# Attention and ternary FFN sandwich on one core: a second pair's bias written into PSUM by VectorE in place of ScalarE

## What is computed

```
x = x + layernorm(attention(layernorm(x)))
x = x + layernorm(ffn(layernorm(x)))

attention: qkv = x @ W_qkv + b_qkv; 16 heads of 8 dims
  scores = q k^T / sqrt(8) + rel_bias[clip(i - j + 128, 0, 256)]   (per head)
  out = softmax(scores) @ v, then @ W_out + b_out
ffn: h = silu(x w1^T s1) * (x w2^T s2); h = gelu(h h1^T s); h = gelu(h h2^T s); h w3^T s
```

## Time and profile before

| what | us |
|---|---|
| median of 3 executions | 339.37 |
| lowest and highest | 337.92, 339.51 |
| the profiled execution: its time | 338.78 |
| the profiled execution: its span in the trace | 337.0 |
| TensorE busy | 282.9 (84%) |
| ScalarE busy | 220.1 (65%) |
| VectorE busy | 210.0 (62%) |
| GpSimd busy | 49.8 (15%) |

### The profile page before, as it was taken

How to read it: one execution, slowest core, us unless ns; L and a number is a source line. 1 busy time by engine, 2 the same in 40 slices (tenths; PEclk the granted TensorE clock), 3 DMA queues, 4 the chain that set the end, 5 groups by cost and what they waited for, 6 DMA issues and landing times.

```text
span 337.0 us, 4914 instructions
## 1 busy us (share of the span) xinstructions
PE 282.9 (84%) x1778; PEld 181.2 (54%) x1778; DVE 210.0 (62%) x444; ACT 220.1 (65%) x315; POOL 49.8 (15%) x51
## 2 busy tenths in 40 slices
PE   0787979999999899999989967838788997999960
PEld 0454545455555465555555533425567876788840
DVE  4666644425967869686785945923857733655454
ACT  1297056447688795987879699615594867687640
POOL 6302300000100101000010137201403200401011
PEclk9999555559999999999999995585997999999995
DMA  6955891102222052341312000000000000010102
GB/s 163 372 179 139 241 330 19 58 15 80 66 65 93 21 177 63 102 153 42 90 32 66 3 1 2 0 5 0 1 0 2 0 0 0 2 31 1 33 1 62
DMA packets 22731, 22.85 MB, mean 68 GB/s; under 512 B 4017, under 2 KB 19505, under 8 KB 22449
## 3 DMA queue, kind: packets, MB, share of 16 engines
q1 hardware_dynamic: 19872, 19.16, 18.6%
q10 hardware_dynamic: 2832, 3.34, 3.1%
HBM read 15.93 MB, written 6.29 MB: 66 GB/s over the span
## 4 chain that ended last, share of the span: by engine, by line
PE 46%; DVE 24%; ACT 12%; issue 8%; SPq 6%; DMA 3%; POOL 1%; POOLq 0%; ACTq 0%; DVEq 0%
PE place L1066 8%; DVE mx L514 8%; PE place L1067 8%; PE place L918 6%; PE pv L966 6%; ACT ring L744 5%; PE place L910 3%; SPq L340 3%; DVE stats L461 3%; ACT place L751 3%; PE place L944 3%; DVE place L521 2%; PE pv L1067 2%; PE pv L1066 2%; DVE y_and_z L472 2%
## 5 line engine op out<-in xcount | busy, mean ns | idle before, releaser
L514 DVE TENSOR_REDUCE mx<-place 128x4 f32<-128x1024 f32 x64 | 78.2, 1223 | 43.3 <-PE place L918 43.3
L744 ACT ACTIVATE ring<-place 128x1024 f32<-128x1024 f32 x64 | 65.2, 1020 | 6.3 <-PE place L955 4.5
L751 ACT COPY place<-raw 128x1024 f32<-128x1024 f32 x48 | 48.8, 1016 | 18.1 <-DVE mx L514 18.1
L918 PE MATMUL place<-room,identr 128*128 128x512 f32 x128 | 54.0, 507 | 0.0
L406 POOL TENSOR_TENSOR rstd<-mv,mhalf 128x2 f32<-128x2 f32 (+1 forms) x24 | 20.4, 848 | 206.4 <-DVE mv L469 206.4
L944 PE MATMUL place<-room 33*128 33x256 f32 x256 | 36.3, 365 | 6.7 <-ACT place L751 4.3
L966 PE MATMUL pv<-ring,vx 128*9 128x256 f32 x512 | 38.7, 426 | 1.0 <-ACT ring L744 1.0
L1066 PE MATMUL place<-room,w_hi 128*128 128x512 f32 x96 | 38.6, 402 | 0.5 <-DVE room L623 0.5
L910 PE MATMUL place<-room 33*128 33x256 f32 x256 | 32.6, 335 | 7.6 <-ACT ring L744 5.2
L623 DVE TENSOR_TENSOR room<-ring,room 128x512 fp32r<-128x512 f32 x32 | 21.7, 691 | 26.2 <-ACT room L831 26.2
L1067 PE MATMUL place<-room,w_hi 128*128 128x512 f32 x96 | 37.7, 393 | 0.0
(11 more groups left out here) (97 smaller groups left out, 391.6 us busy)
## 6 DMA issues: line engine op xcount, KB each, us to landing
room<-q_parts SPq DMA_DIRECT2D x64, 64.0 KB
room<-k_parts SPq DMA_DIRECT2D x64, 64.0 KB
raw<-ext ACTq DMA_DIRECT2D x4, 768.0 KB, 8.0
w_lo<-h SPq DMA_DIRECT2D x2, 1024.0 KB, 5.1
k_parts<-z_parts SPq DMA_DIRECT2D x6, 256.0 KB, 3.1
k_parts<-w_hi SPq DMA_DIRECT2D x6, 256.0 KB, 3.9
xs<-x SPq DMA_DIRECT2D x4, 256.0 KB, 5.8
q_parts<-z_parts SPq DMA_DIRECT2D x4, 256.0 KB, 3.3
```

The costliest lines, as they stand in the source:

```text
L514: nc.vector.tensor_reduce(mx[:, s // RPAIRS, :, :, s % RPAIRS].rearrange("p i k -> p k i"), tile_of(b * PAIRS + s)[:, :, :].rearrange("p k ...
L744: nc.scalar.activation(probs[:, s % PRING, :, :, :].rearrange("p k j n -> p (k j n)"), tile_of(b * PAIRS + s)[:, :, :].rearrange("p k n -> ...
L751: nc.scalar.copy(tile_of(i)[:, :, :].rearrange("p k (j n) -> p k j n", j=2), pair_windows(raw[:, :, :], i % PAIRS)).then_inc(bias_set, 1)
L918: last = mm(tile_of(b * PAIRS + s)[:, half, :], identr[:, :], windows(table_hi[:, 2 * s + half, :], 0, P, 2, S), start=False, stop=True, s ...
```

## The change

Pair 2 of each batch joins pair 5: VectorE copies its bias, ScalarE does not. Everything else, TensorE's program, GpSimd's and the DMA queue's included, has the same instructions in the same order.

```
-BY_DVE = (5,)
+BY_DVE = (2, 5)
```

## The result

| | us |
|---|---|
| before, median of 6 executions | 339.53 (337.92 to 345.63) |
| changed, median of 6 executions | 331.53 (330.23 to 338.53) |
| ratio | 0.9756, 95% interval 0.9717 to 0.9795 |
| the changed kernel's profiled execution: time, span | 338.53, 336.7 |

The sign was right, the size was not: 8 us for the 2.5 forecast. One thing must be said to read any of these numbers: executions of either kernel fall into two groups some 6 us apart, and a median of six moves with the count in each.

A forecast was written before the change was run, and what follows sets the result against it. No engine is full; a loop of waits through ScalarE's copy of pair 2 sets the 20.19 us batch. Gains 1.4 + 0.2 + 0.95 = 2.5 us, from a mean of 338.9, give 336.4 us, range 334.6 to 338.9.

The forecast's parts named there:

- What VectorE has to bear: Slot 0 of a batch: the new 1.23 us copy fits VectorE's 1.40 us gap, 0.14 to spare, and costs nothing.
- What ScalarE wins: Batches 1 to 6: pair 1's exponential starts near 139.0, not 139.8; slot 2's maximum matmuls follow sooner, 0.27 us off TensorE's path.
- what is late next: Slot 4: maximum matmuls still wait for pair 3's exponential, so L540 waits for project; 0.23 us a batch remain, 1.4 for six.
- Batch 0: First batch, at half clock: the step from score to maximum matmuls shortens; gain taken as 0.2 us.
- Batch 7: Last batch, ScalarE full: the removed copy shortens the path by its full step, 0.95 us, bounds 0.33 and 1.0.
- only the ends gain: Rival, batches 1 to 6: another wait holds the period at 20.19; gain 0.95 + 0.2, 337.7 us; chance 0.17.
- The clock eats it: Rival, FFN: started 2.5 us earlier, it meets one more clock dip, at most 1.8 us lost, 338.2 us; chance 0.08.
- VectorE becomes the bound: Rival, gap of slot 0: a copy over 1.37 us delays the reduction of slot 1; 341.1 us at 1.9; chance 0.06.
- The clock holds in the last batch: Rival, batch 7: with less waiting TensorE might keep 2.4 GHz, 1.3 us more gain, 335.1 us; chance 0.07.
- Batch 0 runs at half clock: First batch: assumed at half clock, where the step is 0.73 against 0.59 unwaited; the 0.2 us gain rests on it.

The follow-up runs named there:

- e11: The changed kernel with VectorE writing the bias of pair 2 twice in a row; 337.25 us in its one execution, period 20.99 us.
- e3: The kernel before with the copy of pair 2 on VectorE in batches 1 to 6 alone; median 338.02 us.
- e7: The changed kernel a third time, nothing altered, beside the kernel before; median 334.75 us, ratio 0.9938; its profiled execution took 330.26 us.
- e1: The changed kernel a second time, nothing altered, beside the kernel before; median 336.34 us, ratio 1.0084.
- e9: The changed kernel with VectorE writing pairs 2 and 4 in place of 2 and 5; median 335.66 us, ratio 0.9867 to the kernel before.

## Why the prediction was right or wrong

The mechanism of the waits and nearly their sum were right, the level was not.

- *What VectorE has to bear*: right. Copy 1.23 at its place, no delay behind it, and e11 shows that the next microsecond there would have cost 1.03.
- *What ScalarE wins, what is late next*: right where it decides: 0.34 (0.35) from L944 to L910, L910 in slot 4 held by the exponential (up to 144.94, then 0.14), L540 right behind project, a period of 19.96 (19.96). One term was too small: TensorE's path gained 0.37 and not 0.27 (weighted starts 4.28 behind the reduction of slot 0 and not 4.65), since L910 in slot 2 took 0.50 behind its wait and takes 0.40 without one. The prediction had this 0.1 in its bounds, and it changes nothing, since project is late next. The gain of 0.23 is measured over five periods, 1.15; the sixth is part of the stretch up to the first L540.
- *Batch 0*: not told apart from batch 1; the two together gave 0.2 to 0.5 (0.43). *Batch 7*: 0.94 (0.95) up to the last L540.
- *The rivals*: "only the ends gain" is out by the period. "The clock eats it" came true in size in the first profile, 0.88 back in the last batch and about 0.8 more behind it, but not as an effect of the change (e3 has the 0.88 too, and e7 has neither). "VectorE becomes the bound" didn't, though it was near. "The clock holds in the last batch" named the right kind of cause at the wrong place; no run shows its reason, the shorter waits.
- **The step that failed** is "Batch 0 runs at half clock", taken as a property of the kernel. It is one of that execution. In e7, the same program as the change, the clock rose at 55.6 and the stretch up to the first L540 took 36.11 us in place of 41.87: 5.8 us that the sum had no term for. The three executions of before, with a spread of 1.6 us, had shown none near 333. The range was drawn from these executions and one clock pattern, and so it had no place for 331.
- *Luck*: the forecast of 336.4 is close to what the changed kernel gives when the clock rises late, 336.34 in e1 and a middle value of 336.2 in the upper group below. Two errors nearly cancel there: the level of before, 338.9, was 0.7 below the middle value of its upper group, and the gain of 2.5 is 0.9 below the distance of the upper groups.

How large is the change then? Over all measurements the kernel before had 80 executions, of which 23 at 331.7 to 334.2 and the others from 337.9 up; the changed kernel 24, of which 9 at 329.9 to 332.4 and the others from 334.4 up. Middle value against middle value, the lower groups differ by 3.1 us (333.5 to 330.4), the upper by 3.4 (339.6 to 336.2), the means of all by 3.5 (337.9 to 334.4). So the change is worth some 3 us, about 0.9%, of which the traced waits explain 2.3 to 2.4; the rest, about 1 us, isn't explained. It is smaller than what the same instructions vary by: from L615 to the end of the span the 16 profiles take 114.1 to 116.1 us, the two of the changed kernel that rise late 116.1 and 114.7. The shares in the lower group (23 of 80, 9 of 24) are too close to say that the change makes an early rise more likely. The first ratio of 0.9756 compared four executions of the lower group with five of the upper one.

## What to carry to other kernels

A copy moved to an engine that idles in exactly that place is free, and what it is worth is read from the one chain through it: here an exponential that came 0.8 us earlier left 0.23, because the maximum matmuls of slot 4 wait for another exponential, which starts 6.95 us behind the reduction of slot 0 where it was 6.99. Look at everything queued behind a moved instruction, not only at the next of its kind (e9). And where a profile shows a long stretch at half clock, look at it in several executions before calling it the kernel's: a few times that agree can all be of one kind.

## What the hardware showed that was not expected

In the profile of before TensorE was busy 20.00 of 20.00 us from 46 to 66, and the granted clock stayed at 0.50 until 77.5:

```profile
46.00:56.00 10.00, 10.00 (x54) 5.59 (x56) 3.68 (x3) 6.14 (x9) 0.00 (x0) 0.50 0.47 136
56.00:66.00 10.00, 10.00 (x55) 5.59 (x54) 4.81 (x4) 6.02 (x8) 0.00 (x0) 0.50 0.19 56
```

In e7 it was busy 10.00 of 10.00 from 46 to 56, and the clock rose at 55.6. The same work in the middle batches, with TensorE a little less busy (19.15 of 20.21), ran at 1.00 throughout. The Trainium skill, "TensorE: Matmul & The Clock Gate", section "What's actually happening", has sustained activity release the throttle, and calls the point at which it does so variable from run to run, with a cost of under 1% of a typical span. Here the variation alone was 5.8 us of 337, 1.7%, and a busy TensorE stayed at the lower level for over 30 us: on that the measurement decides.
